# Power on GpSimd for the inverse norms, and the value products at the end of a tick, in a two-layer recurrent block kernel

## The reference, cut to what matters

```
layer 0:  h = layernorm(x)
          a = causal attention(h), 16 heads of 64, then @ Wo + bo
          f = top-1 routed experts (8) + shared expert, SwiGLU, width 352
          x = x + a * silu(f)
layer 1:  h = layernorm(x)
          s = linear attention(h), 16 heads of 8, phi = elu + 1, cumulative sums over tokens
          y = local attention transformer(h), depth 2:
              q, k, v = shift(y) @ wqkv             # 8 heads of 64
              q = q / |q| * q_scale ; k = k / |k| * k_scale ; rotary xpos
              window attention, @ wo, residual
              layernorm(shift(y)) @ w1, gelu gate, @ w2, residual
          x = x + s * silu(y)
layernorm(x) = (x - mean) / sqrt(var + 1e-5)
```

## Time and profile before

| | |
|---|---|
| median of 3 runs | 2353.08 us (2352.51 to 2355.82) |
| profiled execution | 2357.51 us, its span 2355.6 us |
| PE busy | 1896.2 us (80%) |
| DVE busy | 1287.8 us (55%) |
| ACT busy | 1239.2 us (53%) |
| POOL busy | 838.0 us (36%) |
| granted TensorE clock, mean | 0.904 |

### The profile page before, as it was taken

One profiled execution on the slowest core, in us unless ns is written; L12 is line 12 of the kernel. 1 busy time (PEld: TensorE's weight loads), 2 busy tenths in 40 slices (PEclk: granted clock), 3 DMA queues, 4 the chain that ended last, 5 costly groups with the idle time before them and its releaser, 6 DMA issues.

```text
span 2355.6 us, 34690 instructions
## 1 busy us (share of the span) xinstructions
PE 1896.2 (80%) x10900; PEld 1178.0 (50%) x10900; DVE 1287.8 (55%) x4083; ACT 1239.2 (53%) x3559; POOL 838.0 (36%) x912
## 2 busy tenths in 40 slices
PE   5599987986798878986899679976898779857866
PEld 4378754553355345553456335543555436534534
DVE  4345446545655546555754564545654565556644
ACT  2455545653565556555555555554664456445434
POOL 2722234324432433224431343224332443244431
PEclk9799999997899988998999799997899789968878
DMA  7155400000000000000000000000000000000000
GB/s 222 45 182 155 143 19 5 1 1 5 1 1 15 4 2 1 15 1 1 5 10 5 1 1 1 19 1 1 1 10 5 1 1 1 6 4 1 5 0 5
DMA packets 49711, 53.26 MB, mean 23 GB/s; under 512 B 6386, under 2 KB 42236, under 8 KB 49532
## 3 DMA queue, kind: packets, MB, share of 16 engines
q0 software_dynamic: 7808, 27.79, 3.5%
q1 hardware_dynamic: 41724, 23.26, 3.4%
HBM read 41.60 MB, written 9.44 MB: 22 GB/s over the span
## 4 chain that ended last, share of the span: by engine, by line
PE 52%; DVE 17%; ACT 15%; issue 12%; POOL 4%; DMA 1%; DVEq 0%; SPq 0%; ACTq 0%; POOLq 0%
PE ps L551 5%; PE ps L595 5%; PE ps L567 4%; PE ps L543 4%; PE ps L520 4%; PE ps L540 3%; DVE big L1163 3%; ACT p L811 3%; ACT p L812 3%; PE ps L669 2%; DVE p L974 2%; ACT big L888 2%; PE ps L511 2%; PE ps L530 2%; PE ps L715 2%
## 5 line engine op out<-in xcount | busy, mean ns | idle before, releaser
L811 ACT ACTIVATE p<-p,nmax 128x128 f32<-128x128 f32 x512 | 201.7, 394 | 421.4 <-DVE nmax L974 420.8
L669 PE MATMUL ps<-wqkv,hT 128*128 128x512 f32 x384 | 224.8, 699 | 137.4 <-ACT big L889 87.7
L974 DVE CUSTOM_DVE_ANT_0 p<-ps,mask,nrq 128x128 f32<-128x128 f32 (+1 forms) x512 | 182.7, 412 | 215.6 <-PE ps L543 215.3
L1377 POOL TENSOR_TENSOR big<-big,rots 128x512 f32<-128x512 f32 x64 | 132.5, 2070 | 385.7 <-DVE ss L1158 375.6
L551 PE MATMUL ps<-ident,p 128*128 128x128 f32 x1536 | 248.3, 300 | 10.9 <-DVE ff L1021 4.9
L974 DVE CUSTOM_DVE_ANT_0 p<-ps,mask 128x128 f32<-128x128 f32 (+1 forms) x512 | 152.2, 353 | 186.2 <-PE ps L543 171.2
L1273 POOL COPY rdx<-rden 128x256 f32<-128x256 f32 x256 | 95.0, 400 | 446.3 <-DVE rden L990 446.2
L812 ACT ACTIVATE p<-p,nmax 128x256 f32<-128x256 f32 x512 | 252.4, 493 | 0.0
L551 PEld LDWEIGHTS ps<-ident,p 128*128 128x128 f32 x1536 | 179.6, 150 | 109.3 <-issue 93.3
L669 PEld LDWEIGHTS ps<-wqkv,hT 128*128 128x128 f32 x384 | 69.7, 210 | 249.8 <-ACT big L889 144.0
L530 PE MATMUL ps<-ident,big 128*128 128x128 f32 x512 | 93.9, 326 | 123.8 <-DVE big L1168 79.1
(11 more groups left out here) (214 smaller groups left out, 4049.1 us busy)
## 6 DMA issues: line engine op xcount, KB each, us to landing
slots_in<-xn SPq DMA_DIRECT2D x1, 2560.0 KB, 13.7
v<-slots_in SPq DMA_DIRECT2D x20, 128.0 KB, 4.8
slots_out<-v SPq DMA_DIRECT2D x20, 128.0 KB, 1.8
big<-in_x SPq DMA_DIRECT2D x4, 512.0 KB, 6.4
x<-in_x SPq DMA_DIRECT2D x8, 256.0 KB, 3.7
out_x<-x SPq DMA_DIRECT2D x8, 256.0 KB, 2.3
wqkv<-in_wqkv SPq DMA_DIRECT2D x2, 768.0 KB
xn<-in_x SPq DMA_DIRECT2D x6, 256.0 KB, 3.3
```

The costliest lines, as they stand in the source:

```text
L669: MM(bank[:, :], c.hT[:, t * P:(t + 1) * P], c.wqkv[:, l, i * INNER1:(i + 1) * INNER1], start=True, stop=True).then_inc(c.mm_full, 1)
L811: A(p[:, 0:P], p[:, 0:P], ACT.Exp, bias=c.nmax[:, u % 4, 0:1], scale=-1.0, accum_out=den[:, 0:1])
L974: last = V.tensor_tensor_reduce(out=c.p[:, u % 4, a:b], in0=bank[:, a:b], in1=c.mask[st.kind][:, P * (1 - i):SEQ], scale=scale, scalar=3e3 ...
L1377: G.tensor_tensor(dst[:, :, :, 0:H2], src[:, :, :, H2:HD], tab[:, :, :, 0:H2], ALU.mult)
```

## The change

Three things are changed in the text.

First, `newton_rsqrt` and the DVE stages `ln1n`, `ln2n` and `rr` are gone. POOL computes the same values with a power of -1/2: an addition or a maximum, then one `tensor_tensor` with `ALU.pow` whose second operand is a [128, 1] tile of -0.5, broadcast. This is done on 4 columns for each `ln1n`/`ln2n`, on 64 for each `rr`, and on 32 once at the start. POOL waits on the semaphore of its own instruction between them.

Second, the semaphores follow. `moments` on DVE increments `mv_ready`, which POOL awaits, in place of waiting for itself. `nrq` and its increment of `r_ready` are made by POOL; `kn` on DVE and POOL awaits `r_ready` as before. At the start DVE awaits POOL's `rstd_ready` before it whitens.

Third, on PE `values` and `merge` stand after the side stages of the tick, and on ACT the evacuation of `merge` does; in the ring `mm` the unit of `merge` comes after the side stages' units.

```diff
-def newton_rsqrt(nc, link, r, v, scratch):
...
@@ moments
-    link(last)
+    last.then_inc(c.mv_ready, 1)
@@ count_units
-        if st := plan.step(tick - 2):
-            if st.s == 0:
-                o.add(("o", st.pair))
-            else:
-                mm.add(("m", st.pair))
+        if (st := plan.step(tick - 2)) and st.s == 0:
+            o.add(("o", st.pair))
         for seg in plan.side.get(tick, ()):
...
+        if (st := plan.step(tick - 2)) and st.s:
+            mm.add(("m", st.pair))
@@ tensor, the loop over the ticks
-        if st := plan.step(tick - 2):
-            values(st)
-            if st.s == 1:
-                merge(st.pair)
...
         for seg in plan.side.get(tick, ()):
             if seg[0] in stage:
                 stage[seg[0]](*seg[1:])
+        if st := plan.step(tick - 2):
+            values(st)
+            if st.s == 1:
+                merge(st.pair)
@@ scalar, the loop over the ticks: merge(st.pair) likewise after the side stages
@@ vector
-    def ln1n(b):
-        inverse_root(nc, link, c)
-        dve.sem_inc(c.rstd_ready, 1)
-    def rr(b, l):
-        g = LAYERS * b + l
-        dve.wait_ge(c.ss_ready, TILES * (g + 1))
-        link(TS(c.ss[:, :], c.ss[:, :], 1e-24, None, ALU.max))
-        newton_rsqrt(nc, link, c.rr[:, :], c.ss[:, :], c.scratch[:, 0, :])
-        TS(c.nrq[:, l, :, :], ..., -8.0, None, ALU.mult).then_inc(c.r_ready, 1)
@@ gpsimd
+    def inverse_root():
+        link(G.tensor_scalar(c.rstd[:, :], c.mv[:, :, 1], 1e-5, None, ALU.add))
+        link(G.tensor_tensor(c.rstd[:, :], c.rstd[:, :], c.mhalf[:, 0:1].to_broadcast([P, TILES]), ALU.pow))
     def ln1n(b):
-        pool.wait_ge(c.rstd_ready, plan.whitened[("ln1n", b)])
+        pool.wait_ge(c.mv_ready, plan.whitened[("ln1n", b)])
+        inverse_root()
...
+    def rr(b, l):
+        g = LAYERS * b + l
+        pool.wait_ge(c.ss_ready, TILES * (g + 1))
+        link(G.tensor_scalar(c.rr[:, :], c.ss[:, :], 1e-24, None, ALU.max))
+        link(G.tensor_tensor(c.rr[:, :], c.rr[:, :], c.mhalf[:, 0:1].to_broadcast([P, TILES * 2 * HEADS1]), ALU.pow))
+        q = c.rr[:, :].rearrange("p (t a h) -> p t a h", t=TILES, a=2)[:, :, 0, :]
+        G.tensor_scalar(c.nrq[:, l, :, :], q, -8.0, None, ALU.mult).then_inc(c.r_ready, 1)
...
+    link(G.tensor_scalar(c.rstd_all[:, :], c.mv_all[:, :, 1], 1e-5, None, ALU.add))
+    G.tensor_tensor(c.rstd_all[:, :], c.rstd_all[:, :], c.mhalf[:, 0:1].to_broadcast([P, ALL]), ALU.pow).then_inc(c.rstd_ready, 1)
+    pool.wait_ge(c.rstd_ready, 1)
```

More of the change, by code:

```diff
@@ L39 @@
 XRING = 3
-RSQRT_MAGIC = 1597463007.0
 KN_VECTOR = 2
@@ L281, in moments @@
         last = nc.vector.bn_aggr(c.mv[:, t, :], c.stats[:, t, :])
-    link(last)
-def inverse_root(nc, link, c):
-    link(nc.vector.tensor_scalar(c.scratch[:, 0, 0:TILES], c.mv[:, :, 1], 1e-5, None, ALU.add))
-    newton_rsqrt(nc, link, c.rstd[:, :], c.scratch[:, 0, 0:TILES], c.scratch[:, 1, 0:TILES])
+    last.then_inc(c.mv_ready, 1)
 def whiten(eng, out, x, mv, rstd, t):
@@ L378, in buffers @@
     c.rstd = sb("rstd", [P, TILES])
+    c.mhalf = sb("mhalf", [P, 1])
     c.scratch = sb("scratch", [P, 2, 64])
@@ L408, in buffers @@
         sem(n + "_loaded") for n in ("const", "wqk", "wo", "sh", "p1"))
+    c.rstd_ready = sem("rstd_ready")
     c.stats_ready, c.xr_ready, c.xr_pool_ready, c.hot_ready, c.best_ready, c.best_sig, c.gate_ready, c.pos_ready = (
@@ L418, in buffers @@
     c.xag_ready, c.hn_ready, c.fin_th, c.out_ready = (sem(n) for n in ("xag_ready", "hn_ready", "fin_th", "out_ready"))
-    c.rstd_ready, c.prod_ready, c.sum_ready = (sem(n + "_ready") for n in ("rstd", "prod", "sum"))
+    c.mv_ready, c.prod_ready, c.sum_ready = (sem(n + "_ready") for n in ("mv", "prod", "sum"))
     c.x0_loaded = sem("x0_loaded")
@@ L936, in scalar @@
             copies(plan.step(tick - 1))
-        if (st := plan.step(tick - 2)) and st.s == 1:
-            merge(st.pair)
         if tick == 4:
@@ L944, in scalar @@
                 stage[seg[0]](*seg[1:])
+        if (st := plan.step(tick - 2)) and st.s == 1:
+            merge(st.pair)
 def vector(nc, dve, c, plan, mm, s, pt, o):
@@ L1121, in ln2 @@
         moments(nc, link, lambda t: c.h[:, t, :], c)
-    def ln2n(b, l):
-        inverse_root(nc, link, c)
-        dve.sem_inc(c.rstd_ready, 1)
     def phi(b, t):
@@ L1168, in rot @@
         TT(c.qkr[:, t, :], c.qkr[:, t, :], c.sq[:, t % 2, :], ALU.add).then_inc(c.rot_ready, 1)
-    def rr(b, l):
-        g = LAYERS * b + l
-        dve.wait_ge(c.ss_ready, TILES * (g + 1))
-        link(TS(c.ss[:, :], c.ss[:, :], 1e-24, None, ALU.max))
-        newton_rsqrt(nc, link, c.rr[:, :], c.ss[:, :], c.scratch[:, 0, :])
-        TS(c.nrq[:, l, :, :], c.rr[:, :].rearrange("p (t a h) -> p t a h", t=TILES, a=2)[:, :, 0, :], -8.0, None, ALU.mult)\
-            .then_inc(c.r_ready, 1)
     def kn(b, l):
@@ L1207, in vector @@
     stage = {"wo": wo, "ffn": ffn, "down0": down0, "comb": comb, "route": route, "tables": tables, "eg": eg, "ln1": ln1,
-             "ln1n": ln1n, "ln2": ln2, "ln2n": ln2n, "phi": phi, "sum": total, "o1": o1, "s1": s1, "qkv": qkv, "rot": rot,
-             "rr": rr, "kn": kn, "glu": glu, "down1": down1, "fin": fin}
+             "ln2": ln2, "phi": phi, "sum": total, "o1": o1, "s1": s1, "qkv": qkv, "rot": rot,
+             "kn": kn, "glu": glu, "down1": down1, "fin": fin}
     for i in range(4):
@@ L1218, in vector @@
     link(last)
-    var, tmp = c.few[:, 0:ALL], c.few[:, ALL:2 * ALL]
-    link(TS(var, c.mv_all[:, :, 1], 1e-5, None, ALU.add))
-    newton_rsqrt(nc, link, c.rstd_all[:, :], var, tmp)
     dve.sem_inc(c.stats_ready, 1)
+    dve.wait_ge(c.rstd_ready, 1)
     for i in range(BLOCKS):
@@ L1353, in ln2n @@
     def ln2n(b, l):
-        pool.wait_ge(c.rstd_ready, plan.whitened[("ln2n", b, l)])
+        pool.wait_ge(c.mv_ready, plan.whitened[("ln2n", b, l)])
+        inverse_root()
         for t in range(TILES):
@@ L1392, in gpsimd @@
     stage = {"scatter": scatter, "wg": wg, "r": r, "xn": xn, "tables": tables, "lin": lin, "kv": kv, "qkv": qkv,
-             "kn": kn, "shift": shift, "cum": cum, "ln1n": ln1n, "ln2n": ln2n}
+             "rr": rr, "kn": kn, "shift": shift, "cum": cum, "ln1n": ln1n, "ln2n": ln2n}
+    link(pool.memset(c.mhalf[:, :], -0.5))
     pool.memset(c.zero[:, 0, :], 0.0).then_inc(c.zero_ready, 1)
```

## The result

The changed kernel takes 2435.55 us (median of 4 runs, 2434.73 to 2436.47), the kernel before 2352.8 us in the same comparison: a ratio of 1.035, 95% interval 1.0332 to 1.0368. It is 83 us slower, where 50 us less was forecast.

The account below looks back on a forecast made before the run. PE, DVE and ACT were taken to hand the chain on from tick to tick. Terms of 10 + 18 + 14 + 25 = 67 us, counted at three quarters, 50 us, gave 2303 us (own range 2286 to 2326; 8-in-10 range 2248 to 2362).

Parts of the forecast that it names:

- the price of the power: POOL's power in place of Newton: 2.0 us taken for 64 columns, 0.35 us for 4.
- rival 1: Power on POOL is dear: decides from 6.5 us on; at 10 us 60 us lost, 2413 us; chance 14%.
- The row that I took as an end of the range: POOL's two-input products: eleven Newton steps at that price, 3.7 us for 64 columns, as the power's upper end.
- Newton leaves DVE: Newton sequences on DVE: 111 us less work there, of which 88 us lie on the chain.
- My discount of a quarter: Whole sum: three quarters of 67 us counted, 50 us, because the next path is often close.
- rival 4: DVE's 88 us of Newton and 50 us of rT waits leave the chain: 104 us gained, 2250 us; chance 12%.
- ln1n and ln2n: Layernorm stages moved to POOL: 14 us gained, 0.7 us for each of 14 on the chain plus 4 us.
- what remains counts only where the mask ended last: In ln1n/ln2n, DVE reaches the next mask 2.4 us sooner, counting only where the mask ended last; 0.7 us each.
- Value products last: Values and merge after PE's side stages, rT's evacuation later on ACT: 25 us gained, 14 in qkv ticks, 11 elsewhere.
- rr at both depths: The rr stage moved to POOL: 10 us gained in 8 cases at depth 1, 18 us in 7 at depth 0.
- The points of no gain: In rr, loss begins at a power over 3.2 us at depth 1 and 4.6 us at depth 0.
- The lock: Power keeps DVE's two-input instructions out for its 2 us in 15 rr: 15 us less gain, 2318 us; chance 10%.

Follow-up runs that it names:

- the split: Changed kernel with rr's power split: k's 32 columns before kn, q's 32 two ticks later; 2361.7 us beside 2353.4 for the kernel before.
- The kernel by tile: Changed kernel with rr's power made 16 columns at a time after POOL's products in each qkv tick; 2313.0 us beside 2353.6 for the kernel before.
- without the price: Changed kernel with the powers of rr, ln1n and ln2n replaced by multiplications by a constant; 2262.4 us beside 2353.6 for the kernel before.

## Why the prediction was wrong

- **The step that failed is the price of the power.** I took 2.0 us for 64 columns, between POOL's plain product and eleven plain steps (3.7 us), and it is 10.55. My reason for 2.0 (a logarithm, a product and an exponential) is shown by no run; they show only the durations. The mechanism was right: rival 1 put the time with a power of 10 us at 2413, with 15 us for each further microsecond, and the split measured 14.5. With that slope the 8.55 us that the price was short are 124 us; taken off 2435.6 they leave 2311.6. This is an estimate beyond the two prices that the slope is from. The kernel by tile, with 2.92 us of power just before `kn`, came to 2313.0 us. That 2311.6 comes near the forecast of 2303 is in part luck: two other terms were off, in opposite directions (below). The row that I took as an end of the range was no bound, and I gave the case beyond it 14% and left it out of the range.
- **Newton leaves DVE.** The removed work was right in direction; DVE's busy time fell by 88 us, not 111: the 111 held the joins between the instructions, which are not busy time, and `kn` on DVE grew from 25.0 to 33.4 us. The worth of it was undervalued: without the price 91 us came back in total, with the order worth nothing or less. My discount of a quarter did not show; that is rival 4's first half.
- **ln1n and ln2n.** I had 14 us; alone they give 39, although the power on 4 columns costs 1.04 us and not 0.35. The step "what remains counts only where the mask ended last" was too small: the 14 Newton sequences on the chain, 2.4 us each, are 34 us together, and more than that came back when merge stood ahead of the wait. The prediction also held TensorE's clock fixed, and it rose from 0.904 to 0.921. With the merge behind the wait, as in the changed kernel, this gain was not measured by itself.
- **Value products last.** The sum of 25 us was 14 for the `qkv` ticks and 11 elsewhere. The `qkv` ticks alone gave 25, the other ticks alone lost 17, and in all ticks nothing is gained. I saw that loss, and only charged it against the gain of ln (1.5 us in 13 ticks), not to the order itself.
- **rr at both depths.** The points of no gain (3.2 and 4.6 us of power) were not measured. The split does not contradict them: with 5.44 us before `kn`, which is beyond both, the kernel is 8 us slower than before, although it has the gain of the layernorms in it.
- **The lock.** The power does not keep DVE out. The 1.22 us that I added for the collision with `rot` do show, as a longer maximum (1.40 us for 0.33).
- **The clock.** No term had it. It is higher in the kernels that gain most (0.924 without the price) and lower in the changed one (0.898). In the changed one PE was not busy longer for it (1872.1 us for 1896.2), so no part of the 83 us is shown to be the clock's.

## What to carry to other kernels

Before an operation moves to another engine, its own row on that engine has to exist; the rows of plain operations are no bound for a function, and where a wait with a whole engine behind it takes the price, one microsecond in 16 places cost 14.5 us. A dear operation can still pay if it is cut up and put where its engine waits: by tile it ran longer in sum and the kernel was 123 us faster. An order "last in a tick" gained in the ticks where another engine held the path and lost where PE waited, so it is to be decided tick by tick. And the granted clock belongs beside every time: a wait that gets shorter can bring it back, and one kernel's runs can differ by it.

## What the runs showed of the hardware

- A power on GpSimd (`tensor_tensor` with `pow`, float32, second operand broadcast) takes 0.40 us and 159 ns a column: 1.04 us for 4, 2.92 for 16, 5.44 for 32, 10.55 for 64 columns, within 0.5% for 16 columns and more and within 1.4% for 4, unless it starts during a two-input instruction of VectorE (3.33 to 3.84 us for 16). A product of 64 columns takes 0.29 us.
- A `rot` (two inputs of 1024 columns on VectorE) runs at full speed inside a power (1.21 us, 7 cases), whereas beside GpSimd's products it takes 2.17 us.
- With the granted clock at its lower level (0.5) four products of the probabilities with v took 1.12 us, at the upper 0.65. The clock fell during a wait of PE of 3.27 us and stayed up in a wait of 2.72 us at the same place of another kernel.
- One kernel's runs took 2275.8 to 2279.3 us at a mean granted clock of 0.924 to 0.927 and 2295.7 to 2296.4 us at 0.916.
